# Routed expert tiles: each tile's addition issued ahead of a later tile's gather, a third column of row weights, and the last tile's halves interleaved with its predecessor

## The reference, cut to what matters

```python
logits = _gelu(x @ rw1) @ rw2
probs = jax.nn.softmax(logits, axis=-1)
wgt, idx = jax.lax.top_k(probs, TOP_K)          # 2 of 8 experts
for e in range(E):
    Ye = _gelu(x @ w1[e] + b1[e]) @ w2[e] + b2[e]      # 256 -> 1024 -> 256
    Ce = _gelu(b1[e]) @ w2[e] + b2[e]
    for k in range(TOP_K):
        mask = idx[..., k] == e
        out = out + active * wgt[..., k:k + 1] * where(mask[..., None], Ye, Ce)
x = x + jnp.tanh(g_ffn[1]) * out
```

## Time and profile before

| | before |
|---|---|
| median of three runs | 411.5 us |
| the profiled execution's own time | 412.41 us |
| its span in the trace | 410.6 us |
| PE busy | 321.0 us, 78% of the span |
| DVE busy | 306.0 us, 75% |
| ACT busy | 268.2 us, 65% |
| POOL busy | 180.4 us, 44% |
| 23 gathers on POOL | 22.8 us busy |
| 23 additions on POOL | 36.4 us busy |

### The profile page before, as it was taken

How to read it: one execution, slowest core, us unless ns; L and a number is a source line. 1 busy time by engine, 2 the same in 40 slices (tenths; PEclk the granted TensorE clock), 3 DMA queues, 4 the chain that set the end, 5 groups by cost and what they waited for, 6 DMA issues and landing times.

```text
span 410.6 us, 8728 instructions
## 1 busy us (share of the span) xinstructions
PE 321.0 (78%) x2708; PEld 222.1 (54%) x2709; DVE 306.0 (75%) x745; ACT 268.2 (65%) x540; POOL 180.4 (44%) x245
## 2 busy tenths in 40 slices
PE   0075989989799986878777224698999999999991
PEld 0053337664377654556444113475777777777760
DVE  4998997783954663897998885586777777888760
ACT  1825766725676486989798665652677777777770
POOL 3051305391384067433747459410444554444432
PEclk9997999989989998999977756697999999999997
DMA  5950002851095069130416449455677777778522
GB/s 176 388 222 0 2 0 107 126 147 59 4 225 158 15 85 221 46 117 2 119 42 206 126 102 329 154 219 177 184 254 248 255 200 255 210 253 254 154 26 26
DMA packets 27298, 60.48 MB, mean 147 GB/s; under 512 B 4305, under 2 KB 17954, under 8 KB 24066
## 3 DMA queue, kind: packets, MB, share of 16 engines
q1 hardware_dynamic: 20658, 53.20, 40.2%
q0 software_dynamic: 4416, 6.13, 9.3%
q10 hardware_dynamic: 2192, 0.75, 0.7%
HBM read 29.00 MB, written 6.85 MB: 87 GB/s over the span
## 4 chain that ended last, share of the span: by engine, by line
PE 42%; DVE 28%; DMA 10%; issue 9%; ACT 8%; POOL 2%; ACTq 1%; SPq 0%; DVEq 0%; POOLq 0%
PE bank L1270 8%; PE bank L1637 6%; PE bank L1655 6%; DMA out_dram<-arena,SI 5%; DVE MX L2000 3%; PE bank L1640 3%; PE bank L1658 3%; DMA STG<-in_l_w_dram 2%; PE bank L1356 2%; PE bank L1231 2%; DMA arena<-NMS 2%; PE bank L1382 2%; DVE stats L1720 2%; PE bank L1378 1%; ACT arena L1131 1%
## 5 line engine op out<-in xcount | busy, mean ns | idle before, releaser
L1655 PE MATMUL bank<-arena 128*128 x184 | 63.4, 390 | 2.6 <-DVE X L2274 1.1
L1131 ACT ACTIVATE arena<-arena,B1D 128x128 f32<-128x128 f32 x184 | 57.4, 391 | 8.6 <-DVE arena L2287 8.1
L2287 DVE TENSOR_REDUCE arena<-bank 128x256 f32<-128x512 f32 x92 | 57.3, 680 | 3.1 <-PE bank L1640 3.1
L685 POOL TENSOR_TENSOR W<-STG,W 128x256 f16<-128x256 f32 x64 | 42.7, 700 | 33.4 <-ACT W L882 28.9
L782 POOL DMA_INDIRECT out_dram<-arena,SI x23 | 36.4, 1584 | 36.2 <-DMA out_dram<-arena,SI 16.9
L1658 PE MATMUL bank<-arena 128*128 x184 | 51.3, 279 | 0.0
L685 POOL TENSOR_TENSOR arena<-STG,arena 128x256 f16<-128x256 f32 x56 | 37.3, 700 | 30.2 <-ACT arena L882 28.8
L1637 PE MATMUL bank<-arena 128*128 128x256 f16 x256 | 46.4, 282 | 1.6 <-DVE arena L2250 1.6
L769 POOL DMA_INDIRECT arena<-token_rows,GI x23 | 22.8, 993 | 53.3 <-ACT WS L1125 45.1
L2292 DVE SCALAR_TENSOR_TENSOR arena<-arena 128x512 f16<-128x512 f32 x46 | 29.7, 688 | 21.8 <-ACT arena L1138 21.8
L1640 PE MATMUL bank<-arena 128*128 128x128 f16 x256 | 45.3, 225 | 0.0
(11 more groups left out here) (280 smaller groups left out, 722.3 us busy)
## 6 DMA issues: line engine op xcount, KB each, us to landing
STG<-in_l_w_dram SPq DMA_DIRECT2D x32, 512.0 KB, 4.0
arena<-W SPq DMA_DIRECT2D x16, 1024.0 KB
STG<-W SPq DMA_DIRECT2D x7, 1024.0 KB
arena<-in_l_w_dram SPq DMA_DIRECT2D x2, 1280.0 KB, 7.5
k_parts<-W SPq DMA_DIRECT2D x2, 768.0 KB, 4.4
arena<-k_parts SPq DMA_DIRECT2D x12, 128.0 KB, 5.2
X<-in_x_dram SPq DMA_DIRECT2D x2, 512.0 KB, 7.4
W<-in_ctx_dram SPq DMA_DIRECT2D x1, 1024.0 KB, 10.2
```

The costliest lines, as they stand in the source:

```text
L685: ins = nc.gpsimd.tensor_tensor(l, src, h, ALU.subtract)
L1131: ins = nc.scalar.activation(x, x, ACT.Gelu, bias=B1D[:, e, c:c + 1], scale=1.0 / (X_SCALE * W_SCALE))
L1655: nc.tensor.matmul(bank[6 + q][:, :], GDL[:, q, 0, c * P:(c + 1) * P], W2[:, e, c].rearrange("p s d -> p (s d)"), start=(c == 0), stop=Fal ...
L2287: v.tensor_reduce(half, o, AX.X, ALU.add).then_inc(s_dadd, 1)
```

## The change

The change has three parts.

1. `gather_rows(j + 4)` stands behind `add_to_out(j)` from j = 2 on. For j = 0 and 1 the old order is kept.
2. `WS` has three columns, and a tile uses column j mod 3. ACT may then write tile j's column when tile j-3's result is done.
3. For tile 22 ACT issues the first high half after four pieces of GELU, then two more pieces, `low_out` of tile 21, the last two pieces and the second high half. DVE issues `tile_out` of tile 21 between the two low halves of tile 22.

```diff
-        WS = sb("WS", [P, 2], F32)
+        WS = sb("WS", [P, 3], F32)
...
             for j in range(TILES):
-                if j + 4 < TILES:
+                if j < 2:
                     gather_rows(j + 4)
                 add_to_out(j)
+                if 2 <= j < TILES - 4:
+                    gather_rows(j + 4)
...
-            def tile_gelu(j, q, m, first=False):
+            def tile_gelu(j, q, m, y, first=False, last=False):
...
                 if not first:
-                    act.wait_ge(s_ysa, j - 1)
-                    act.wait_ge(s_ys, j - 1)
-                nc.scalar.activation(WS[:, q:q + 1], XRG[:, q, bass.ds(e, 1)], ACT.Copy).then_inc(s_ws, 1)
+                    act.wait_ge(s_ysa, j - 2)
+                    act.wait_ge(s_ys, j - 2)
+                nc.scalar.activation(WS[:, y:y + 1], XRG[:, q, bass.ds(e, 1)], ACT.Copy).then_inc(s_ws, 1)
...
+                gelu(0, 4).then_inc(s_dg, 1)
+                if last:
+                    hidden_high(0)
+                    gelu(4, 6)
+                    low_out(j - 1, 1 - q, (j - 1) % 3)
+                    gelu(6, 8).then_inc(s_dg, 1)
+                else:
+                    gelu(4, 8).then_inc(s_dg, 1)
+                    hidden_high(0)
+                hidden_high(1)
...
-                for hb in range(2):
-                    split_hidden(j, j % 2, hb)
-                tile_out(j - 1, (j - 1) % 2, (j - 1) % 3)
+                split_hidden(j, j % 2, 0)
+                if j == TILES - 1:
+                    tile_out(j - 1, (j - 1) % 2, (j - 1) % 3)
+                split_hidden(j, j % 2, 1)
+                if j < TILES - 1:
+                    tile_out(j - 1, (j - 1) % 2, (j - 1) % 3)
```

More of the change, by code:

```diff
@@ L1132, in tile_gelu, with hidden_high @@
                                                    scale=1.0 / (X_SCALE * W_SCALE))
-                    ins.then_inc(s_dg, 1)
-                for hb in range(2):
+                    return ins
+                def hidden_high(hb):
                     act.wait_ge(s_dg, 2 * j + hb + 1)
@@ L1155, in _ @@
                 for r in range(UNROLL):
-                    tile_gelu(UNROLL * i + HEAD + r, (HEAD + r) % 2, UNROLL // 2 * i + (HEAD + r) // 2)
+                    tile_gelu(UNROLL * i + HEAD + r, (HEAD + r) % 2, UNROLL // 2 * i + (HEAD + r) // 2,
+                              (HEAD + r) % 3)
                     low_out(UNROLL * i + HEAD + r - 1, (HEAD + r - 1) % 2, (HEAD + r - 1) % 3)
             for j in range(TAIL, TILES):
-                tile_gelu(j, j % 2, j // 2)
-                low_out(j - 1, (j - 1) % 2, (j - 1) % 3)
+                tile_gelu(j, j % 2, j // 2, j % 3, last=j == TILES - 1)
+                if j < TILES - 1:
+                    low_out(j - 1, (j - 1) % 2, (j - 1) % 3)
             low_out(TILES - 1, (TILES - 1) % 2, (TILES - 1) % 3)
@@ L2296, in tile_out @@
                 dve.wait_ge(s_ysa, j + 1)
-                v.scalar_tensor_tensor(out=YS[:, y], in0=bank[6 + q][:, 0:D], scalar=WS[:, q:q + 1], in1=YS[:, y],
+                v.scalar_tensor_tensor(out=YS[:, y], in0=bank[6 + q][:, 0:D], scalar=WS[:, y:y + 1], in1=YS[:, y],
                                        op0=ALU.mult, op1=ALU.add).then_inc(s_ys, 1)
```

7 lines of the change are left out of this document (4 added, 3 removed).

## The result

The changed kernel takes 428.5 us, median of 6 runs (427.7 to 431.3). Beside it the kernel before takes 412.2 us (6 runs, 410.2 to 417.2). It is 4.2% slower, where the prediction said 1.6% and a range up to 421.5. The direction was right and the size was not.

A forecast was written before the change was run, and what follows sets the result against it. PE, busy for the whole loop, was taken as the bound. First late gather 1.8, loop 5.6, tail -0.7 sum to +6.7 us: 419.1 against the profiled 412.41, given as 418 us, 1.6% slower, range 410.6 to 421.5.

The forecast's parts named there:

- What bounds the kernel: Tiles 6 to 22: PE alone sets the pace, 5.46 us a tile, and whatever makes it wait adds in full.
- Addition j can start 0.75 us after the end of tile j, if its predecessor has landed: Additions on POOL in the new order: addition 18 at 383.75 instead of 386.60, addition 20 at 394.64 instead of 395.80.
- rival C: Loop: the weight block catches the addition too, the gather waits behind both; 1.6 us per two tiles, 423.8 us, chance 0.12.
- The ring: PE's loop from transpose j+2 to transpose j+4, through gather j+4: spans two tiles, forecast at 11.7 rather than 10.93 us.
- The gather behind the block: Loop, tiles 8 to 20: each gather waits for the whole weight block, 0.8 us late per two tiles, 5.6 us in all.
- The first gather: Gather 6, behind late addition 2: starts at 300.25 at the soonest, PE waits 1.8 us (bounds 0.8 and 2.5).
- Three columns at nothing: Third column of WS: costed at nothing, but without it the gather could not run ahead of its tile's result.
- The last tile and the tail: Tiles 21 and 22: tile 21 ends sooner, tile 22 later, last addition at 403.95 instead of 404.69; gain 0.7 us.
- The rule that spoke against it: DMA engines take turns between queues packet by packet, so a gather would pass most of the weight block, not late.
- Rival B: Start of addition 2: addition 1 lands ahead of its tile's weight block, loop costs nothing; 410.0 to 410.8 us, chance 0.14.
- Rival A: Loop: gathers slip between the weights, not held back; only gather 6 may cost; 412.6 us, lower bound 411.6, chance 0.22.
- rival D: Last tile: tile 21's `low_out` holds GELU longer, tile 22 ends beyond the additions; each us costs one; no separate chance.

## Why the prediction was wrong

Its steps in their order:

- **What bounds the kernel: right.** The loop had no slack on PE. Each us that PE waits is in the time.
- **"Addition j can start 0.75 us after the end of tile j, if its predecessor has landed": the step that failed.** The condition did not hold for tiles 3 to 14. I had the late start of addition 2 in hand (298.37) and used it for gather 6, but then let addition 3 start from the end of its tile, as if the chain had caught up. The trace of before had the answer: each of its additions 2 to 17 was issued 0.45 to 1.67 us after the first packet of the block, so each was held and made the next one late. Additions 3 to 18 start 1.1 to 1.4 us after the last packet of their predecessor, though the timeline calls most of these waits "issue". Nothing in the change moved the block or addition 2. The lateness of the chain, harmless before, became the lateness of the gathers: they cost 1.14 us a tile up to tile 17, where the forecast had 0.4.
- **Behind the block there are then two transfers, not one.** That is the mechanism of rival C. It was given 1.6 us for two tiles and 0.12. The ring measured is 13.2 us for two tiles on average (2 x 72.67 / 11), 2.3 above 10.93. C was short at least in part since I counted 2.4 us for a block, from its rate; from first packet to last it takes 3.1 to 3.8.
- **The gather behind the block, the forecast's own mechanism: right in its cost, where the additions are on time.** The pairs of transposes 17 and 19, 18 and 20, 19 and 21 are 11.93, 11.76 and 11.82 us apart; 11.7 was forecast. Started after a wait, POOL takes 0.28 us and not 0.75, so the gather starts 2.19 us after the end of tile 18 (403.98 - 401.79), not 2.64; the block starts 3.45 to 3.6 us after the end, not 3.7. PE has the rows 7.6 to 7.8 us after it, not 7.3. The forecast had these gathers wait for the whole block; they share it and end with it (see the rule below).
- **The first gather: right.** Forecast: 0.30 us after addition 2, PE waits 1.8. Measured: 303.49 is 0.30 after 301.61 + 1.58, and transpose 6 is 1.69 late.
- **PE's restart: missing.** 3.9 us of issue before the up products of tiles 10 and 16, of which writing the loop out gave back 2.4. I had assumed that an engine that waits loses only the wait.
- **Three columns at nothing: right** (the kernel with the old order). That the new order needs them was wrong (the order on POOL alone, with two).
- **The last tile and the tail: right in sign, -1.2 us instead of -0.7.** Tile 21 ends 9.25 us after tile 22's transpose, which is the forecast to the hundredth (398.75 - 389.50), and tile 22 13.34, forecast 13.5. The last addition starts 14.02 us after the transpose, where 14.45 was forecast. The difference is the 0.28 in place of 0.75 at tile 21; the last addition waits for its predecessor, as forecast.

The ledger of the profiled execution, tile 5 to the last addition: +1.7 at tile 6; +12.6 from tile 6 to 17, in which waits for gathers are 6.1, the two restarts 3.9, and PE being busier 2.6 (62.68 against 11 x 5.46), which no run explains; +1.9 from tile 17 to 22; -1.2 in the tail. That makes +15.0. The forecast had 1.8 + 5.6 - 0.7. With its own slope right and the state wrong for eleven tiles, the error lies in the second term, 14.5 us where 5.6 was forecast.

**The rule that spoke against it.** In the late state an addition issued 0.20 us before the first packet of a block has no packet for 2.9 us while queue 1 has 100.1% of the engines. In the on-time state gather 19 is issued by 385.91 + 1.01 = 386.92, 0.28 us ahead of the block, and 18 packets of queue 0 move among 60 of queue 1 from 387.9 to 389.5. Yet that doesn't bring it through early; its last packets come at the block's end.

The Trainium skill (DMA: Bandwidth & Descriptors, section Queues, rings and completion order) has each engine take turns between queues packet by packet, and by a packet it means some 9 to 17 descriptors, which an engine drains before it switches. I had taken the profile's packets for these, and that a gather would pass most of the block doesn't follow from the rule. A block is 128 packets of 8 KB in the profile, 8 for each of the 16 engines. If each is one descriptor, which no run here shows, they are fewer than the 9 to 17, and the rule lets a whole block through ahead of an addition, as in the late state. The gathers that share a block it doesn't explain.

**Rival B** named the race with the block, for addition 1 and its tile alone. It was lost there, and the same race is run again in each tile. **Rival A** is out by the waits at ten transposes, and **rival D** didn't come: the last addition is not bound by the end of tile 22.

Three things stay open.

- What takes the chain out of the late state at tile 15. In the traces it is the restart of PE's loop before the up product of tile 16, which holds PE and the next block back by 2 us while addition 14 goes ahead. The restart at tile 10, of 1.85 us, was not enough: it left addition 8 only 0.25 us ahead of its block. With the loop written out the chain also got out, at tile 12, after transpose 11 had waited 2.66 us, and with the new order from tile 12 on after a wait of 1.71 us. Any long enough stop of PE at the right place would explain these, and no run was made with such a stop alone.
- Why the restart takes 2 us. PE reads the expert's number twice there. In the changed kernel the reads take 0.88 and 0.94 us at tile 10 and 1.01 and 1.15 us at tile 16, while a block of weights is moved; in the kernel before they take 0.30 us each, and so do reads in the changed kernel when no block moves. And the branch back, 0.22 to 0.24 us long in both kernels, comes 0.24 to 0.35 us after the start of the transpose before it in the kernel before, and 1.3 to 1.4 us after it in the changed kernel, where PE's instructions had stood at that transpose until its rows were there. Together that makes the 2.2 to 2.6 us by which PE is ready later for the up product, enough for the idle time of 1.85 and 2.02. This was read from traces and not tested by itself.
- Why some gathers share a block. In four traces (the changed kernel, the order on POOL alone, PE's loop written out, the new order from tile 12) ten gathers were issued 0.27 to 0.48 us ahead of a block. Nine of them had their first packet 0.9 to 1.4 us after the issue, one after 2.3. Of eight issued 0.08 to 0.25 us ahead seven waited 1.7 to 2.9 us. The changed kernel's three additions at 0.20 to 0.30 us waited 3.1 to 3.2.

## What to carry to other kernels

Where one engine issues two kinds of transfers in turn, putting one behind the other hands it all the lateness of the first, and the lateness is to be followed through the chain tile by tile, not set to zero after the first. A chain that runs late at no cost can begin to cost: look for what depends on it after the change. If a small transfer races a long one on another queue, look at which of the two comes first in each tile and by how much; the race can have two lasting states. Here cutting the long one in two settled it, and giving what depends on the small one a buffer more made its loss harmless.

## What was unexpected of the hardware

- A 1 MB transfer, once it has its first packets, holds an addition, an indirect DMA of another queue, nearly until its end: 2.9 us without a packet at tile 13. In tiles 2 to 13 of the changed kernel the addition's first packet comes 0.5 to 1.0 us before the block's last one ends. Where it doesn't meet a block, the first packet comes 0.57 us after the issue ends (tiles 14 and 15).
- The addition had to be issued 1.39 us or more ahead of the block for the next one to be on time. 1.16 us was not enough once (tile 7 of the kernel with the order alone): its first packets came ahead of the block, 0.57 us after the issue, its last only at the block's end (336.1), and its successor started 3.54 us late.
- POOL starts 0.28 us after the result that it waits for, when it waits for DVE. The 0.75 that I had read from the chain holds for a wait for its own DMA.
- A loop on PE that goes back right behind a transpose that had to wait costs 1.2 to 2.2 us; before the change there is no gap at these tiles. In one case of five the granted clock was at its lower level behind it for some 3 us, which cost 1.7 us more.
